# Negated score maxima as three rows of the stacked queries, brought by transfers

## The reference

```
x += band attention(norm(x))      # 16 heads of 64, window of 128
x += ffn0(norm(x))                # int8 weights, 384 hidden
x += causal attention(norm(x))    # 16 heads of 8
x += ffn0(norm(x))
x += chunk attention(norm(x))     # 16 heads of 8, chunks of 64 tokens
x += ffn1(norm(x))                # fp4 blocks of 16, 352 hidden
x += lowrank attention(norm(x))   # 16 heads of 8, no mask
x += ffn1(norm(x))
```

## Time and profile before

| | |
|---|---|
| median of 3 runs | 2169.54 us (2167.63 to 2172.38) |
| profiled execution | 2175.12 us, span 2173.3 us |
| granted TensorE clock, mean | 0.930 |
| busy: PE, DVE, POOL, ACT | 82%, 63%, 44%, 37% |
| selector products (nmT, pick) | 2560 matmuls, 217.6 us of records |

### The profile page before, as it was taken

The page is one execution under the profiler, slowest core; times in us unless marked ns, Lnnn a source line. Parts: engine busy times, 40 slices in busy tenths (PEclk is TensorE's granted clock), DMA queues, the critical chain, the costliest instruction groups (busy, mean ns, idle before and its releaser), DMA issues.

```text
span 2173.3 us, 51626 instructions
## 1 busy us (share of the span) xinstructions
PE 1791.2 (82%) x21261; PEld 1259.5 (58%) x21261; DVE 1366.8 (63%) x2749; ACT 803.1 (37%) x1298; POOL 961.6 (44%) x1266
## 2 busy tenths in 40 slices
PE   2899999999999998878999987777776777777774
PEld 2566666666666666655555556666665455555553
DVE  5744445555455553565555555678777688888875
ACT  0233333333333332324444443333433444444442
POOL 1522223333322323443434345589886455555533
PEclk7999999999999999989999999879888788888987
DMA  4000000000000000023333323233332222232210
GB/s 159 1 2 1 1 2 1 1 1 1 1 1 1 2 1 1 16 59 74 70 78 71 77 60 74 46 83 82 79 85 60 59 55 57 64 64 64 58 27 8
DMA packets 167464, 89.54 MB, mean 41 GB/s; under 512 B 9393, under 2 KB 165810, under 8 KB 166978
## 3 DMA queue, kind: packets, MB, share of 16 engines
q1 hardware_dynamic: 167010, 85.70, 17.1%
q0 software_dynamic: 224, 0.54, 0.1%
HBM read 46.36 MB, written 39.85 MB: 40 GB/s over the span
## 4 chain that ended last, share of the span: by engine, by line
PE 48%; DVE 35%; issue 6%; ACT 5%; POOL 2%; DVEq 0%; DMA 0%; POOLq 0%; SPq 0%; ACTq 0%
PE slots L1302 34%; DVE nmx L1194 13%; PE ctx_ps L1302 9%; DVE rope_part L1235 6%; DVE rope_part L1159 2%; PE slots L1577 2%; ACT ctxT L1000 1%; DVE band_r L1160 1%; DVE band_va L626 1%; DVE ctxT L1278 1%; DVE band_va L629 1%; ACT probs L1080 1%; DVE rope_part L1160 1%; ACT band_va L1000 1%; DVE band_va L624 1%
## 5 line engine op out<-in xcount | busy, mean ns | idle before, releaser
L1194 DVE TENSOR_REDUCE nmx<-slots 128x8 f32<-128x1024 f32 (+2 forms) x352 | 407.9, 1216 | 107.9 <-PE slots L1302 104.7
L1080 ACT ACTIVATE probs<-slots 128x1024 f32<-128x1024 f32 (+1 forms) x416 | 356.0, 892 | 302.4 <-PE slots L1302 299.2
L1302 PE MATMUL slots<-band_r 64*64 64x64 bf16 (+4 forms) x5120 | 392.4, 262 | 85.3 <-DVE nmx L1194 42.4
L1302 PEld LDWEIGHTS slots<-band_r 64*128 64x128 bf16 (+2 forms) x5120 | 192.9, 120 | 254.9 <-issue 126.9
L1235 DVE SCALAR_TENSOR_TENSOR rope_part<-slots,bias_qk,rope_band 128x256 f32<-128x256 f32 x512 | 212.3, 477 | 197.4 <-PE slots L1302 173.3
L1302 PE MATMUL ctx_ps<-probs,band_va 64*32 64x64 f32 (+4 forms) x5120 | 257.0, 312 | 47.6 <-issue 24.5
L979 POOL TENSOR_TENSOR band_r<-rope_part 128x512 f32<-128x512 f32 x128 | 164.3, 1284 | 251.0 <-DVE rope_part L1235 251.0
L1302 PE MATMUL slots<-mask,ident_bf 128*128 128x256 bf16 (+1 forms) x896 | 217.0, 324 | 45.9 <-DVE nmx L1194 16.5
L1302 PEld LDWEIGHTS ctx_ps<-probs,band_va 128*32 128x32 f32 (+2 forms) x5120 | 145.4, 118 | 129.8 <-issue 66.0
L893 POOL TENSOR_TENSOR var_eps<-mean_var,eps 128x2 f32<-128x2 f32 x128 | 29.2, 228 | 430.4 <-DVE mean_var L1122 430.4
L1302 PE MATMUL slots<-nmT,pick 64*128 64x256 bf16 (+2 forms) x2560 | 217.6, 240 | 1.5 <-issue 1.4
(11 more groups left out here) (173 smaller groups left out, 2926.9 us busy)
## 6 DMA issues: line engine op xcount, KB each, us to landing
band_r<-scratch SPq DMA_DIRECT2D x192, 192.0 KB, 4.4
scratch<-parts SPq DMA_DIRECT2D x96, 192.0 KB, 2.2
scratch<-parts SPq DMA_DIRECT2D x96, 128.0 KB, 2.1
scratch<-parts SPq DMA_DIRECT2D x96, 64.0 KB, 1.9
x<-in_x SPq DMA_DIRECT2D x16, 128.0 KB, 2.8
out<-x SPq DMA_DIRECT2D x16, 128.0 KB, 1.8
band_r<-in_band_qk_a SPq DMA_DIRECT2D x1, 1024.0 KB, 6.3
band_r<-in_band_qk_b SPq DMA_DIRECT2D x1, 1024.0 KB, 7.9
```

The costliest lines, as they stand in the source:

```text
L1080: nc.scalar.activation(probs[:, g % 2, step[2], :, 0:width], slot(u, step).rearrange("p (a n) -> p a n", a=2)[:, :, 0:width], ACT.Exp, sca ...
L1194: nc.vector.tensor_reduce(dst, src, axis=AX.X, op=ALU.max, negate=True).then_inc(free_sem(u, step), 1)
L1302: return nc.tensor.matmul(o, lhsT, rhs, start=start, stop=stop, skip_group_check=shared)
```

## The change

The small attentions' `nm` step moves from the back stage to the end of the maxima stage. Its three parts go into `nm3` with the even heads in one half and the odd in the other (`by_half`), so that after the transpose and the copy each half of `nmT` has 24 rows, 3 parts times 8 heads. Two transfers on SP's queue move them to rows 48 to 50 of each half of `stack[0]`. The key stack holds ones in its rows from 48 on (`stack[1]`), so the key product itself adds the maximum and the selector products are dropped. The band attention keeps its own way. For the first scores rows 48 to 50 of the queries must be zero, so a seventh term of zeros in the scratch tensor, written once, is loaded with each query stack, 51 rows instead of 48. The zeroing at the start becomes three memsets, and all constants of the planner (`LEAD`, `PER_UNIT`, settling times) are new.

```diff
 def maxima_steps(kind):
-    return [("score", i) for i in range(SCORE_FILLS[kind])] + [("parts",)] * (kind != "end")
+    return [("score", i) for i in range(SCORE_FILLS[kind])] + [("parts",)] + [("nm",)] * (kind in SMALL)
 def back_steps(kind):
-    steps = [("nm",)]
+    steps = [("nm",)] if kind == "band" else []
...
-        "nm": [("pe", 0.12), ("act", 0.28)],
-        "S": [("pe", {"band": 0.99 if narrow else 1.74, "causal": 0.55 if narrow else 0.8, "chunk": 0.52, "lowrank": 0.48}.get(kind)),
+        "nm": [("pe", 0.12), ("act", 0.28)] + [("sp", 1.3)] * (kind in SMALL),
+        "S": [("pe", {"band": 0.99 if narrow else 1.74, "causal": 0.32 if narrow else 0.5, "chunk": 0.3, "lowrank": 0.24}.get(kind)),
...
-SETTLE = {"pe": 0.18, "act": 0.12, "dve": 0.1, "pool": 0.08, "sp": 4.0}
+SETTLE = {"pe": 0.18, "act": 0.12, "dve": 0.1, "pool": 0.08}
+LANDS = {"stack": 4.0, "nm": 2.2, "res": 1.4}
...
-PER_UNIT = 0.01
+PER_UNIT = 0.0012
...
-        scratch = nc.dram_tensor("scratch", [2, TERMS, P, TOK], BF16, kind="Internal").ap()
+        scratch = nc.dram_tensor("scratch", [2, TERMS + 1, P, TOK], BF16, kind="Internal").ap()
...
+                    if step == ("nm",):
+                        released(sp, u, step)
+                        for half in range(2):
+                            src = nmT[HALF * half:HALF * half + 3 * SD]
+                            sp.dma_start(stack[0][HALF * half + KROWS:HALF * half + KROWS + 3, b % RING], src).then_inc(nm_moved, 16)
...
+                    if s == 0:
+                        sp.dma_start(scratch[0, TERMS], stack[0][:, 0, 0, :]).then_inc(no_rows, 16)
+                        sp.wait_ge(no_rows, 16)
...
+                        used = KROWS + 3 if qk == 0 else KROWS
                         for half in range(2):
-                            sp.dma_start(stack[qk][64 * half:64 * half + KROWS, b % RING],
-                                         rows[:, half::2, :]).then_inc(stack_loaded, 16)
+                            sp.dma_start(stack[qk][HALF * half:HALF * half + used, b % RING],
+                                         rows[0:used, half::2, :]).then_inc(stack_loaded, 16)
...
-                        nc.gpsimd.memset(band_flat[:, 0:2 * half_r], 0.0).then_inc(stack_zeroed, 1)
+                        link(nc.gpsimd.memset(stack[0], 0.0))
+                        link(nc.gpsimd.memset(stack[1][32:HALF], 1.0))
+                        nc.gpsimd.memset(stack[1][HALF + 32:P], 1.0).then_inc(stack_zeroed, 1)
...
+                    if kind in SMALL and name == "nm":
+                        n = FRONT_NO[u, step]
+                        act.wait_ge(front_full, n + 1)
+                        if u == BATCH:
+                            act.wait_ge(back_full, last_exp(u - 1) + 1)
+                        else:
+                            act.wait_ge(nm_moved, 32 * sbase[u])
+                        copy(nmT[:], slot(u, step).bitcast(BF16)[:, 0:TOK]).then_inc(free_sem(u, step), 1)
...
-                    if f == 0 and g == 0:
+                    if f == 0 and g == 0 and kind == "band":
                         released(pe, u, ("nm",))
+                    elif f == 0 and g == 0:
+                        pe.wait_ge(nm_moved, 32 * (sbase[u] + 1))
...
-                                mm(bank(F, h)[out_at, at:at + width], key[:, key_at], q[:, q_at], not opened, False, shared=True)
-                        for h in pair:
+                                last = mm(bank(F, h)[out_at, at:at + width], key[:, key_at], q[:, q_at], not opened, kind != "band", shared=True)
+                        for h in pair if kind == "band" else ():
```

More of the change, by code:

```diff
@@ L174, in needs @@
         if name == "S" and step[1] == 0:
-            yield u, ("nm",), "act"
+            yield u, ("nm",), "act" if kind == "band" else "sp"
         if name == "V":
@@ L225, in needs @@
             yield u, ("xT", step[1]), "pe"
+        if name == "nm" and kind in SMALL:
+            yield (u - 1, ("nm",), "sp") if u > BATCH else (u - 1, LAST_S["band"], "pe")
         if name == "cast" and kind == "band":
@@ L288 @@
     "pe": {
[L289 to L294, removed]
+        "tail": {"band": -1.623, "causal": 78.659, "chunk": 8.708, "lowrank": -0.879},
@@ L295 @@
+        "finish": {"causal": -2.124, "chunk": -0.74, "lowrank": 0.407, "end": -0.81},
+        "forward": {"causal": 11.265, "chunk": -0.452, "lowrank": 0.102, "end": -1.376},
+        "operands": {"band": 19.899, "causal": 11.203, "chunk": 12.533, "lowrank": 57.289},
+        "maxima": {"band": 24.825, "causal": -0.194, "chunk": 0.248, "lowrank": -1.423},
+        "back": {"band": -2.804, "causal": -0.387, "chunk": -0.483, "lowrank": -1.417},
     },
     "act": {
-        "tail": {"band": 53.895, "causal": 17.872, "chunk": 17.73, "lowrank": 16.182},
@@ L298 @@
[L298 to L301, removed]
+        "tail": {"band": 34.709, "causal": 54.632, "chunk": 21.135, "lowrank": 4.853},
+        "finish": {"lowrank": -19.621, "end": -57.621},
+        "forward": {"causal": -22.984, "chunk": 24.376, "lowrank": 4.91, "end": 39.745},
@@ L302 @@
+        "operands": {"band": -1.989, "causal": 6.226, "chunk": -9.162, "lowrank": -16.809},
+        "maxima": {"causal": 10.614, "chunk": -2.295, "lowrank": 32.981},
+        "back": {"band": -0.348, "causal": -21.015, "chunk": 63.002, "lowrank": -6.754},
     },
     "dve": {
-        "tail": {"band": 24.321, "causal": 37.26, "chunk": 2.316, "lowrank": -0.51},
-        "finish": {"causal": -16.196, "chunk": -16.754, "lowrank": -16.243, "end": -0.226},
-        "forward": {"causal": 0.613, "chunk": 33.846, "lowrank": 11.755, "end": -4.652},
@@ L307 @@
-        "operands": {"band": 33.419, "causal": -10.053, "chunk": 2.99, "lowrank": 16.104},
-        "maxima": {"band": 32.94, "causal": 14.633, "chunk": 16.275, "lowrank": 22.45},
+        "tail": {"band": 16.931, "causal": 68.836, "chunk": 2.885, "lowrank": -2.057},
+        "finish": {"causal": -48.569, "chunk": -27.534, "lowrank": 2.298, "end": -8.917},
+        "forward": {"causal": 20.864, "chunk": 45.817, "lowrank": 30.316, "end": -28.767},
+        "operands": {"band": 38.071, "causal": -16.436, "chunk": 2.957, "lowrank": 10.795},
@@ L309 @@
+        "maxima": {"band": 5.428, "causal": -1.149, "chunk": 4.879, "lowrank": 35.713},
     },
     "pool": {
[L311 to L315, removed]
-    },
-}
@@ L318 @@
-PER_UNIT = 0.01
+        "tail": {"band": -14.297, "causal": 45.896, "chunk": -12.11, "lowrank": -18.372},
+        "finish": {"causal": -39.952, "chunk": -104.978, "lowrank": 7.763, "end": 63.046},
+        "forward": {"causal": -25.785, "chunk": -13.853, "lowrank": 14.099, "end": 17.645},
+        "operands": {"band": 32.294, "causal": -42.938, "chunk": 55.73, "lowrank": 34.734},
+        "maxima": {"band": 11.199, "causal": 10.788, "chunk": 12.669, "lowrank": 58.217},
+    },
+}
+PER_UNIT = 0.0012
@@ L321, in released_by, with settles @@
+def settles(step, eng):
+    return LANDS[step[0]] if eng == "sp" else SETTLE[eng]
 def released_by(u, step):
@@ L417, in make_plan @@
         free[eng] = start + time
-        done[u, step, eng] = start + time + SETTLE[eng]
+        done[u, step, eng] = start + time + settles(step, eng)
         order[eng].append(("back" if stage in ("back", "tail") else "front", u, step))
@@ L1395, in front_half @@
                         row_scores(u, step)
+                    if name == "nm":
+                        F = take(u, step)
+                        pe.wait_ge(nm_ready, abase[u] + 1)
+                        onto_heads(F, nm3, front_full)
                     if name in ("qk", "v"):
@@ L1536, in onto_heads @@
                                                    src3[:, t].rearrange("p a h -> p (a h)"), ident_bf[:])
-                    last.then_inc(back_full, 1)
+                    last.then_inc(full, 1)
                 def back_half(u, step):
```

33 lines of the change are left out of this document (23 added, 10 removed).

## The result

The changed kernel takes 2241.89 us (median of 4 runs, 2240.57 to 2250.94), the kernel before 2170.96 (4 runs, 2167.63 to 2172.39) beside it: ratio 1.0338, 95% interval 1.0312 to 1.0364. It is slower, by some 71 us. The forecast was 2140, so the prediction was wrong in sign, and its range of 2090 to 2170 doesn't hold the time. The profiled execution took 2250.94 us, the longest of the four, with a span of 2248.8.

What follows compares the result with a forecast made beforehand. TensorE was fullest (82%), but by stage it led causal, three engines shared chunk and VectorE led lowrank. Gains 16 + 6 + 12 less 4 made 30 us: 2175.1 to 2145.1, the median 5.6 lower, so 2140; range 2090 to 2170.

Steps and rivals of the forecast that it cites:

- The slower rival: Small attentions: maxima transfers queued behind stack loads are waited for past causal's 7.9 us; 2223 us (32 units), 2182 (16); chance 0.11.
- Causal and chunk, 16 + 6: Causal and chunk stages: dropping selector products saves 16 us and 6 us on the path.
- The ceiling by pair starts: Small attentions: selector products priced by steps between pair starts, at most 22 + 8 + 38 = 68 us.
- Lowrank, 12: Lowrank stage: dropping selector products saves 0.75 us a unit, 12 us, kept low because VectorE leads.
- Latency of the maxima transfers, 0: Before second scores: transfers take 2.6 to 5.2 us but existing free time covers them; cost 0, far end 125.
- The start, 4: Start of run: three memsets and a waited store delay the first stack 4 to 9 us; partly covered, cost 4.
- The rival of the broken lockstep: Lowrank: new order parts GpSimd and VectorE, tensor-tensor falls from 1.52 to 0.43 us; 32 us gained, 2108; chance 0.18.
- The clock: Causal stage: forecast keeps clock 0.99; its rival has thinner TensorE work lower it to 0.93, 2176 us; chance 0.05.
- the rival's reason: Causal stage: products taken out leave idle gaps in TensorE's work, which throttle its clock; 36 us; chance 0.05.

## Why the prediction was wrong

**The step that failed** is this one: "The query stack's loads carry 51 rows a half for 48: 6% more in a transfer that scores don't start on at once; nothing." It priced a transfer by its bytes. What it needed was the number of DMA engines that share it, 3 for 16. One load alone then takes 6.1 us for 3.4, and four in a row hold SP's queue 6.7 us, for 3.0 with 56 rows. It cost 81 us, from ratio 0.9964 to 1.0338, more than all other terms together. 49 of them come without any maxima transfer, with TensorE waiting for the stack itself; 33 come with the transfers on the same queue. The fallen clock is in both: 0.95 and 0.91 in causal for 0.98. "Scores don't start on at once" was wrong as well: the kernel before never waits for its stack loads, but with 51 rows and nothing else changed it waits 32.4 us, so the time to spare was less than slow loads add. In the unit shown after, the last load lands 12.6 us after the first is issued (1148.60 to 1161.23); before, the queue's hold of 2.5 and even the longest landing, 5.9, make 8.4.

**The slower rival** was the nearest. It named the place, a maxima transfer queued behind loads, and the point from which it decides, 7.9 us in causal. Here SP's queue needs 6.7 us for the loads, 0.7 for the transfer and 4.7 for its landing, 12.1, and it decided. But the rival had the loads at their old length; with these the run without transfers shows that nothing is lost. Its 2223 left out the wait for the loads themselves, for which no rival stood.

**The sum's other terms.**
- Causal and chunk, 16 + 6: measured 21. The ceiling by pair starts, cut by the share of the unit in which TensorE waits for reduces, gave the right sum; the two stages aren't told apart, as the cut between them moves.
- Lowrank, 12: measured nothing or a loss of some 7. "VectorE leads" was read from the earlier trace rows, and then a gain was booked all the same. VectorE's busy time there is the same with the products and without (354.2 and 355.7 us), and TensorE, with less to do, had a lower granted clock (0.84 and 0.83, the end 0.78 and 0.75). That the clock is the cause was argued, and the run with products in lowrank alone left it open.
- Latency of the maxima transfers, 0: right with quick loads (0.9964 with, 0.9961 without). The free time in the earlier trace rows covers it.
- The start, 4: no run took it apart, but the traces show the parts. With 56 rows the three memsets take 3.54, 3.50 and 3.51 us, so a memset does go by element. The first stack load is issued at 939.4 us for 929.9 before, 9.5 later; in the kernel with only the new order and one memset, at 935.4. With the products kept, the start, the rows of zeros and the transfers together cost some 5 us over the new order alone (1.0027 and 1.0005, intervals that overlap).
- The new order: no gain and no loss (1.0005). The rival of the broken lockstep didn't come: VectorE's tensor-tensor on 256 elements in lowrank takes 1.36 us after, for 1.52, not 0.43.
- The clock: causal was forecast to keep 0.99. In the changed kernel it is 0.91, behind the waits for DMA. In the kernel with 56 rows it is 0.98, with the products or without them, so taking them out did nothing to it, and the rival's reason wasn't at work; first scores over fewer rows did lower it, to 0.92.

Without the failed step the sum is 30 us; the kernel with 56 rows has a median of 2165.5 and 2163.3 in its two runs, 8 to 10 us below the kernel before. Its products brought 14 where 34 were forecast, and lowrank accounts for the difference (12 forecast, some 7 lost). The 4 to 6 us between 14 and 8 to 10 would fit the 4 of the start, but that is the size of the intervals and wasn't tried.

## What to carry to other kernels

Before the row count of a transfer is changed, look at its divisors: some rows of zeros more, up to a count that many DMA engines can share, can be far cheaper than the exact number (56 rows took 3.9 us, 51 took 6.1). On a queue that issues in order, a slow transfer is paid again by each small one behind it. And where another engine leads a stage, work taken off TensorE may bring nothing, as in lowrank here.

## What the hardware showed that was not expected

- Issuing isn't a fixed price. The third load of four is one of keys, of 48 rows as ever, and its issue took 3.38 and 4.04 us in the two units shown, with the slow query loads ahead of it; the longest took 4.7, against 1.5 before.
- A memset by GpSimd took the same time for 4096 elements a partition whatever their type and the number of partitions: 3.50 us for 128 partitions of float32, 3.54 for 128 of bf16, 3.50 for 32 of bf16.
- First scores over 48 rows for 64, of which the rest are zeros, went with a granted clock in causal of 0.92 for 0.98, so with a larger share of its time at 1.2 and not 2.4 GHz, and cost 0.7% of the whole kernel with loads of 56 rows, 0.3% with 48. The Trainium skill ("TensorE: Matmul & The Clock Gate", HAM oscillation) ties a falling clock to idle gaps; here TensorE was idle for 45 us of the stage with the lower clock and 49 with the higher, so more idle time doesn't explain it. What does, no run here shows.
